# The support product of the first layer from fp16 halves of x and W0, in twelve matmuls a tile instead of four fp32 ones

## What is computed

```python
x = _layernorm(x + _L0(x, edge_index, edge_weight, weight, bias))   # support = x @ W0; segment_sum(support[src] * w, dst) + b
x = _layernorm(x + _L1(...))   # two relational layers: w[r] = sum_b att[r, b] basis[b], gates, segment_sum
x = _layernorm(x + _L2(...))   # x @ W, normalised by degree, segment_sum
x = _layernorm(x + _L3(...))   # attention over the edges, 8 heads
```

## Time and profile before

| | us |
|---|---|
| median of 3 runs | 1315.63 |
| lowest and highest | 1310.06, 1317.89 |
| the profiled execution | 1321.34 |
| its span | 1319.6 |
| PE busy in the span | 1223.5 |
| DVE busy in the span | 862.3 |
| ACT busy in the span | 419.5 |

### The profile page before, as it was taken

One profiled execution on the slowest core, in us unless ns is written; L12 is line 12 of the kernel. 1 busy time (PEld: TensorE's weight loads), 2 busy tenths in 40 slices (PEclk: granted clock), 3 DMA queues, 4 the chain that ended last, 5 costly groups with the idle time before them and its releaser, 6 DMA issues.

```text
span 1319.6 us, 22145 instructions
## 1 busy us (share of the span) xinstructions
PE 1223.5 (93%) x8447; PEld 551.8 (42%) x8448; DVE 862.3 (65%) x1178; ACT 419.5 (32%) x564; POOL 309.3 (23%) x220
## 2 busy tenths in 40 slices
PE   6888888899898999999999999989999899999997
PEld 2233333333343333344445443444332455555553
DVE  7475666344334555462478873646999788879787
ACT  2444555322232111212301002125551343334332
POOL 2011010000010243453555655555560000000000
PEclk9988999999998999999999999989999899999999
DMA  8577885598696888745122212113221665556552
GB/s 305 207 235 237 278 288 181 208 371 323 209 368 213 277 273 265 231 117 159 2 49 33 49 21 46 2 2 42 32 32 53 229 219 193 176 177 201 172 173 104
DMA packets 64267, 222.77 MB, mean 169 GB/s; under 512 B 31208, under 2 KB 36072, under 8 KB 48214
## 3 DMA queue, kind: packets, MB, share of 16 engines
q1 hardware_dynamic: 34648, 156.40, 34.8%
q0 software_dynamic: 25184, 53.10, 15.6%
q10 hardware_dynamic: 4350, 12.07, 2.7%
HBM read 198.94 MB, written 59.94 MB: 196 GB/s over the span
## 4 chain that ended last, share of the span: by engine, by line
PE 47%; DVE 8%; issue 6%; DMA 5%; ACT 1%; SPq 0%; DVEq 0%
PE PS L1716 18%; PE PS L1670 6%; PE PS L1955 5%; PE PS L1942 5%; DMA R<-in_basis_s 4%; DVE R L1108 4%; PE PS L1988 3%; PE PS L1975 2%; PE PS L1837 2%; PE PS L1536 2%; DVE R L1143 1%; PE PS L1752 1%; DVE R L1170 1%; PE PS L1641 1%; DMA W<-w_d 1%
## 5 line engine op out<-in xcount | busy, mean ns | idle before, releaser
L749 POOL DMA_INDIRECT bias_d<-R x160 | 271.4, 1696 | 339.6 <-DMA bias_d<-R 224.0
L1716 PE MATMUL PS<-R 128*128 128x512 f16 x1300 | 301.3, 384 | 1.6 <-DVE R L946 1.6
L1716 PEld LDWEIGHTS PS<-R 128*128 128x128 f16 x1300 | 121.2, 98 | 184.7 <-issue 53.6
L1600 PE MATMUL PS<-R,XX 125*128 125x512 f16 (+2 forms) x612 | 131.6, 349 | 26.4 <-DVE R L863 15.3
L1501 ACT ACTIVATE R<-PS 128x1024 f32<-128x1024 f32 (+1 forms) x100 | 100.5, 1005 | 163.4 <-PE PS L1942 163.4
L1143 DVE SCALAR_TENSOR_TENSOR R<-R,W 128x1024 f32<-128x1024 f32 (+1 forms) x68 | 134.3, 1985 | 14.3 <-ACT R L1501 13.1
L1670 PE MATMUL PS<-W,XX 128*128 128x512 f16 x600 | 135.3, 384 | 4.2 <-DVE R L946 2.7
L863 DVE TENSOR_SCALAR R<-W,R 125x1250 f16<-125x1250 f16 x160 | 89.6, 606 | 47.5 <-PE PS L1600 44.1
L1108 DVE CUSTOM_DVE_ANT_0 R<-PS,R 128x1250 f16<-128x1250 f32 x80 | 116.8, 1460 | 5.5 <-PE PS L1889 2.9
L1955 PE MATMUL PS<-R 128*32 128x256 f32 (+1 forms) x1600 | 105.7, 382 | 5.4 <-DVE R L1143 4.8
L1942 PE MATMUL PS<-R 128*128 128x256 f16 (+3 forms) x800 | 105.9, 274 | 1.1 <-DVE R L1108 1.1
(11 more groups left out here) (220 smaller groups left out, 1361.0 us busy)
## 6 DMA issues: line engine op xcount, KB each, us to landing
bias_d<-bias_d POOLq DMA_DIRECT2D x39, 1280.0 KB, 11.5
R<-in_basis_s SPq DMA_DIRECT2D x48, 1024.0 KB, 6.4
W<-bias_d SPq DMA_DIRECT2D x27, 1024.0 KB, 4.9
R<-bias_d SPq DMA_DIRECT2D x13, 1024.0 KB, 4.8
W<-in_basis_s SPq DMA_DIRECT2D x12, 1024.0 KB, 6.0
R<-key_d SPq DMA_DIRECT2D x20, 500.0 KB, 3.8
R<-R SPq DMA_DIRECT2D x120, 80.0 KB, 6.3
W<-bias_d SPq DMA_DIRECT2D x7, 904.0 KB, 4.6
```

Of the source, the lines that this page charges most:

```text
L749: pool.indirect_dma_start(bias_d, bass.IndirectOffsetOnAxis(ap=idx[:, c:c + 1], axis=0), attr[:, c, :], None, bounds_check=DUMP + GC * P - ...
L1600: ins = T.matmul(mm_out(3 * (j % 2) + b, p1 - p0), own[0:EC, bass.ds(c, 1), :, :].rearrange("p c m w -> p (c m w)"), hots(p0, p1), start=f ...
L1716: ins = T.matmul(mm_out(SUM_BANK(s, i), D), lhs, rhs, start=n == 0, stop=n == len(terms) - 1)
```

## The change

x and W0 are split on the chip into an fp16 high half and an fp16 remainder. The four fp32 matmuls of a support tile become twelve fp16 ones: high by high, low by high, high by low. ACT makes the high halves by copies (`W0S[0]`, then one `nodes_high` a tile), DVE the low halves by subtraction (`W0S[1]`, then one `nodes_low` a tile). PE waits for the low halves in place of the loads. The halves lie in buffers that nothing else uses in the preparation.

```diff
@@ DVE, between the table and the edges' keys, and between keys and values
+            def nodes_low(i):
+                dve.wait_ge(x0h_made, i + 1)
+                V.tensor_tensor(XS[:, 1, i, :, :], XTP[:, i, :, :], XS[:, 0, i, :, :], ALU.subtract).then_inc(x0_made, 1)
+
+            dve.wait_ge(w0h_made, 1)
+            V.tensor_tensor(W0S[1], W0P, W0S[0], ALU.subtract).then_inc(w0_made, 1)
+            for i in range(NT // 2):
+                nodes_low(i)
             dve.wait_ge(edges_in, 64)
             step(V.tensor_copy(rowf[0:EC, :], src_i[0:EC, :]))
...
             step(V.scalar_tensor_tensor(key[0:EC, :], parts[0:EC, :], float(NN), rowf[0:EC, :], ALU.mult, ALU.add))
 
+            for i in range(NT // 2, NT):
+                nodes_low(i)
             V.tensor_scalar(valA[0:EC, :, 0], typ_i[0:EC, :], 0, None, ALU.is_equal)
@@ ACT
+            def nodes_high(i):
+                act.wait_ge(xtp_in[i // (NT // 2)], 16)
+                S.activation(XS[:, 0, i, :, :], XTP[:, i, :, :], ACT.Copy).then_inc(x0h_made, 1)
+
...
+            act.wait_ge(w0_in, 16)
+            S.activation(W0S[0], W0P, ACT.Copy).then_inc(w0h_made, 1)
+            for i in range(NT // 2):
+                nodes_high(i)
             for i in range(NT + 1):
+                if i < NT // 2:
+                    nodes_high(NT // 2 + i)
                 if i < NT:
                     first_high(i)
@@ PE
             def first_support(i):
-                if i % (NT // 2) == 0:
-                    pe.wait_ge(xtp_in[i // (NT // 2)], 16)
+                pe.wait_ge(x0_made, i + 1)
                 if i >= 2:
                     pe.wait_ge(sup_made, i - 1)
-                for f in range(FT):
-                    ins = T.matmul(mm_out(6 + i % 2, D), XTP[:, i, f, :], W0P[:, f, :], start=f == 0, stop=f == FT - 1)
+                for n, (p, q) in enumerate(THREE):
+                    for f in range(FT):
+                        ins = T.matmul(mm_out(6 + i % 2, D), XS[:, p, i, f, :], W0S[q][:, f, :],
+                                       start=n == 0 and f == 0, stop=n == 2 and f == FT - 1)
                 ins.then_inc(sup_done, 1)
...
-            pe.wait_ge(w0_in, 16)
+            pe.wait_ge(w0_made, 1)
             pe.wait_ge(minus_made, 1)
```

More of the change, by code:

```diff
@@ L122, in gnn_resnorm @@
         fix16 = in_w(P // 2).bitcast(F16)
+        w0_low = in_w(FT * D // 2).bitcast(F16).rearrange("p (f n) -> p f n", f=FT)
         zero = r3[:, NT * D + 2 * NN + CH:NT * D + 3 * NN + CH]
@@ L174, in gnn_resnorm @@
         W0P = r3[:, NT * D:NT * D + FT * D].rearrange("p (f n) -> p f n", f=FT)
+        XS = r1f[:, NT * NN // 2:NT * NN // 2 + NT * D].bitcast(F16).rearrange("p (q k f n) -> p q k f n", q=2, k=NT, f=FT)
+        W0S = [r1f[:, NT * NN // 2 + NT * D:NT * NN // 2 + NT * D + FT * D // 2].bitcast(F16).rearrange(
+            "p (f n) -> p f n", f=FT), w0_low]
         o = 0
@@ L336, in gnn_resnorm @@
         w0_in = sem("w0_in")
+        w0h_made = sem("w0h_made")
+        w0_made = sem("w0_made")
+        x0h_made = sem("x0h_made")
+        x0_made = sem("x0_made")
         sup_less = sem("sup_less")
```

## The result

The changed kernel takes 1319.57 us (median of 20 runs, 1314.0 to 1323.31), the kernel before 1314.05 us (20 runs, 1309.94 to 1318.21). The ratio is 1.0039 with a 95% interval of [1.0026, 1.0053]: 5.1 us slower, with 3.4 to 7.0 us as the interval. The same pair measured again gave 1.0045 [1.0029, 1.0062]. The time lies in the forecast's range of 1309 to 1326, and "within 1%" is right; of the loss of 5 us the forecast named 1.3. All ratios here leave out three executions that took over 1.5% more than the fastest of their kernel: 1329.84 and 1338.46 us of the kernel before and 2003.62 us of basis first.

What follows compares the result with a forecast made beforehand. PE is busy 93% of the span, but the edit touches only the preparation, ended by PE and ACT. DVE's chain grows 17.5 us against 16.2 of cover: 1315.6 + 1.3 = 1316.9 us, range 1309 to 1326.

Steps and rivals of the forecast that it cites:

- within 1%: Whole kernel: time changes by less than about 13 us either way; chance 0.94.
- The bound of the stage: Preparation ahead of the build: the chain of PE and ACT ends it, DVE having 16.2 us of cover.
- what the change removes: PE's support tiles: 0.80 us less each, 8 us for ten; 9.8 us at most with the 1.78 us pause.
- The later start: PE's first support tile: starts at 17.4 and not at 10.74, 6.7 us later, behind the halves.
- The first tile: PE's first support tile: all twelve matmuls at half speed, 5.1 to 5.3 us, ending at 22.5.
- Rival 2: PE's first tile: full speed from the first matmul, stage 1.2 us shorter, 1314.4 us; chance 0.10.
- DVE held behind ACT's copy of tile 9: DVE's last subtraction: waits for ACT's copy until 36.2, ends at 36.9; `own` ends at 66.7, 1.3 us past the cover.
- Basis 4: Load ahead of PE's mix 4: issued at 41.9, takes 6.4 us, lands at 48.3; PE waits 2.6 us.
- the table's write: SP's queue ahead of basis 4: starts at 39.7 and takes 1.9 us, bounds 1.9 and 7.85.
- a landing behind 50.9: PE's wait ahead of mix 4: basis 4 landing 9.0 us after issue, from which rival 1 decides.
- rival 1: PE's wait ahead of mix 4: basis 4 lands late, PE ends the stage, likelier 1318 to 1324 us; chance 0.18.
- The sum: Preparation stage: PE's chain level or a little shorter, DVE's +17.5 us with 16.2 covered; stage and time +1.3 us.

Runs made afterwards that it cites:

- basis first: Changed kernel with SP issuing basis slices 4 to 7 ahead of the table's trip through DRAM; ratio to the kernel before 1.0018 [0.9998, 1.0039].
- copies first: Changed kernel with ACT's copies of all ten node tiles ahead of its first eviction; ratio to the kernel before 0.9996 [0.9978, 1.0015].
- no remainders: Changed kernel with DVE making no remainders and PE's twelve matmuls a tile all using high halves (wrong product); ratio to the kernel before 0.9957 [0.9935, 0.9980].
- table first: Copies first, with DVE's remainders of tiles 5 to 9 also moved behind the table's last step; ratio to the kernel before 1.0004 [0.9988, 1.0021].
- high products first: Table first, plus basis 4 to 7 ahead of the table and PE's high-by-high products of tiles 0 and 1 ahead of remainders; ratio to the kernel before 0.9987.
- the delayed kernel: Kernel before with three clearings of an unused buffer on DVE ahead of the build; ratio to the kernel before 1.0038 [1.0016, 1.0059].
- before basis first: Kernel before, fp32 matmuls kept, with SP issuing basis 4 to 7 ahead of the table's trip; 1311.2 us, ratio 0.9970 [0.9955, 0.9985].
- splits unused: Changed kernel with all halves made but unread, PE running the four old fp32 matmuls a tile; ratios to the kernel before 0.9984 and, again, 1.0011.
- before, again: Kernel before, unchanged, measured and profiled against itself; ratio 1.0001 [0.9982, 1.0021], profiled execution 1310.23 us.

## Why the prediction was right or wrong

**The bound of the stage, and what the change removes.** Right. The tile is 2.59 us against the 2.64 of the forecast, and PE's pause for the stores went. That at most 0.7% could be won holds: the kernel without remainders won 0.43%.

**The later start.** Right to 0.1 us: 17.37 for 17.4, released by DVE.

**The first tile.** The forecast took 5.1 us of half speed; in both traces of the changed kernel the tile took 3.9 us (21.27 - 17.37), with the last four matmuls at full speed. It differs: in basis first and copies first, with the same start, it took the forecast's 5.07. This is why DVE came 1.3 us earlier than forecast in the changed kernel, and at the forecast's 66.7 in basis first. That the stretch was at half speed is read from the spacing of the matmuls, 0.43 against 0.22 us; the granted clock reads 1.00 in all windows up to 24 us, in every trace. Rival 2, full speed from the first matmul on, did not come.

**DVE held behind ACT's copy of tile 9.** Right, and the central step: its remainder started at 34.95 (36.2 in the forecast), and moving the five copies away removed the wait. `own` ended at 65.38, the forecast had 66.7.

**Basis 4.** Here the forecast failed, in one term and in one omission. The term is the table's write: 1.9 us was taken, as for a small load with nothing ahead of it, and it took 5.07 us (4.41 to 11.34 in the nine other traces with this order of SP, from issue to the read behind it, and 7.4 to 8.0 in the four of them that issued it near 22). It is a write to DRAM, the row chosen was a read into SBUF, and the upper bound, 7.85, was the row of the same write. The load itself took 5.5 us, less than the 6.4. The prediction's other price for it, the estimate of 4.4 us from the Trainium skill (DMA: Bandwidth & Descriptors, section on the anatomy of one DMA), was too low; that section is about transfers that GpSimd issues, and this one was issued by SP. So basis 4 landed at 49.25 and not at 48.3, while PE was ready at 44.6 and not at 45.7, and the wait was 4.70 us and not 2.6. The omission is the clock: the forecast set "a landing behind 50.9" as the point from which rival 1 decides, and counted half speed only beyond it. But the clock fell already with a landing at 49.25, and the 2.35 us behind it bring PE's chain from 49.25 + 15.8 = 65.1 to 67.4 (measured: 67.1), past DVE's 65.4. So **rival 1 came true**, which had 0.18, and by a smaller delay than it was said to need.

**The sum.** For the stage +1.3 us was forecast and +2.0 and +1.8 measured, the right size from the wrong chain, which is luck. For the time +1.3 was forecast and +5.1 and +5.9 measured. That the forecast of 1316.9 still lies within 2.7 us of 1319.57 is luck in part, too: its base, the median of three runs, lay 1.6 us above the median of twenty. If a delay reaches the end one for one, the stage as traced accounts for about 2 of the 5 us. The other 3 us are not settled. Copies first took away 5.6 to 6.4 us of the loss where its stage is 5.6 us shorter, and no remainders 11 to 12 where its stage is 7.2 us shorter. All five kernels in which PE reads remainders lie over what their stages say: changed by 3.1 and 4.1 us, copies first and table first by some 3, basis first and high products first by 1.5 to 2. The lower ends of the intervals are 1.3, 1.9, 0.7 and 0.7, and below nothing for the last two. Of the others, the delayed kernel lies 0.4 over, and no remainders, before basis first and the two of splits unused between 0.7 over and 4.5 under. The stages are from one trace each, and the two of splits unused differ by 1.6 us. The granted clock, listed with every run, is lower in the changed kernel: its mean is 0.980 in both comparisons, against 0.983 to 0.984 in the runs of the kernel before that list it, which is some 6 to 9.5 us more at half speed, of which the fall at 47 us explains 6.8. That leaves at most 2.7 us of half speed, some 1.4 us of time. What the rest is, was not found. No run tests whether it lies in PE's reading of the remainders; splits unused makes them and does not read them, and shows no such loss.

## What to carry to other kernels

When work is added to an engine that has 16 us of cover, ask what else is queued behind it there: not only the large instruction that the cover belongs to, but each semaphore that a third engine waits for. Here a table of 160 bytes stood behind the new subtractions, a DMA queue behind the table, and four loads behind that which have nothing to do with the table; issuing those first costs nothing and gained 0.3% on the old kernel, where the gain came with the end of PE's pause for ACT's stores and not from basis 4, for which that kernel had not waited. A copy that only feeds another engine belongs ahead of evictions that wait for TensorE, since in a written order it otherwise inherits their waits.

## What the runs showed of the hardware

A wait of TensorE of 4.4 to 4.7 us cost another 2.35 to 2.5 us in work at half speed behind it, one of 3.34 us cost 1.65, and one of 2.06 us none. The length of the pause alone does not tell: one of 2.39 us (high products first) cost 1.7 us, with the clock falling 1.1 us after the work had begun again, and one of 2.38 us (before, again) none. A write of 160 bytes to DRAM held its waiting queue for 4.4 to 11.3 us, longest where it was issued 1 us behind copies within DRAM. And the time at half speed in one and the same program ran from 31 to 51 us between two executions whose builds start within 0.12 us, which can be at most 10 of their difference of 11 us.
